# Attention pairs in hardware loops on five engines, in place of straight code

## The reference

```
for i in range(3):
    h  = (x @ W[i]).reshape(n, 4, 32)
    es, ed = einsum(h, att_src[i]), einsum(h, att_dst[i])
    e  = leaky_relu(es[src] + ed[dst], 0.2)
    p  = exp(e - segment_max(e, dst)[dst])
    alpha = p / segment_sum(p, dst)[dst]
    x  = elu(segment_sum(alpha[:, :, None] * h[src], dst) + bias[i])
```

## Time and profile before

| what | value |
|---|---|
| median of 3 runs | 9245.97 us (9245.64 to 9248.44) |
| profiled execution | 9241.63 us |
| its span, first to last instruction | 9239.8 us |
| first attention layer's gathers | 2079 to 4298 us |
| second's | 4450 to 6670 us |
| third's | 6856 to 9025 us |
| instructions executed | 129442 |

### The profile page before, as it was taken

One profiled execution on the slowest core, in us unless ns is written; L12 is line 12 of the kernel. 1 busy time (PEld: TensorE's weight loads), 2 busy tenths in 40 slices (PEclk: granted clock), 3 DMA queues, 4 the chain that ended last, 5 costly groups with the idle time before them and its releaser, 6 DMA issues.

```text
span 9239.8 us, 129442 instructions
## 1 busy us (share of the span) xinstructions
PE 5626.5 (61%) x34288; PEld 4513.0 (49%) x34288; DVE 5638.8 (61%) x13019; ACT 3271.8 (35%) x7522; POOL 5375.1 (58%) x5192
## 2 busy tenths in 40 slices
PE   4999879964555555555455555555534545445456
PEld 3777646653544445444444444454434444444444
DVE  6888721135666666666466666666645555555555
ACT  3555400023333333333343333333323333333334
POOL 2000100047777777775677777777657777777770
PEclk9999989965555555555555555555555555555558
DMA  3333335404444444443344444444423333233321
GB/s 101 136 139 139 125 140 192 175 16 120 119 119 116 122 113 124 114 116 82 96 113 118 119 116 121 113 123 113 104 65 80 85 80 85 79 85 80 85 79 32
DMA packets 601474, 989.07 MB, mean 107 GB/s; under 512 B 331107, under 2 KB 455044, under 8 KB 561524
## 3 DMA queue, kind: packets, MB, share of 16 engines
q0 software_dynamic: 163760, 357.05, 17.1%
q1 hardware_dynamic: 217540, 544.34, 16.8%
q10 hardware_dynamic: 219648, 81.82, 3.4%
HBM read 758.42 MB, written 224.34 MB: 106 GB/s over the span
## 4 chain that ended last, share of the span: by engine, by line
PE 27%; DVE 22%; DVEq 18%; POOL 14%; issue 13%; DMA 5%; ACT 1%; POOLq 0%; SPq 0%; ACTq 0%
DVEq L1264 15%; PE bank L959 13%; POOL arena L649 13%; DVE acc L1866 10%; DMA arena<-row_table,staged_idx 4%; PE bank L1182 3%; PE bank L984 3%; DVE arena L1853 2%; DVE arena L1822 2%; PE bank L1122 2%; DVEq L1866 2%; DVE x_mem L1535 1%; DVE arena L1815 1%; DVEq L1858 1%; PE bank L1247 1%
## 5 line engine op out<-in xcount | busy, mean ns | idle before, releaser
L649 POOL DMA_INDIRECT arena<-row_table,staged_idx x4992 | 5087.9, 1019 | 1626.1 <-issue 1467.3
L1182 PE MATMUL bank<-arena 128*128 128x136 f32 x9984 | 2487.9, 429 | 1207.5 <-DVE acc L1866 1045.8
L1182 PEld LDWEIGHTS bank<-arena 128*128 128x128 f32 x9984 | 2195.9, 316 | 1372.1 <-issue 1231.0
L1866 DVE TENSOR_TENSOR acc<-acc,bank 128x136 f32 x4992 | 1476.7, 296 | 1020.7 <-issue 798.1
L804 ACT ACTIVATE pick_dist<-col,dst_local 128x128 bf16<-128x128 f32 x4992 | 1523.3, 388 | 1092.0 <-PE bank L1182 1091.3
L959 PE MATMUL bank<-arena 128*128 128x385 bf16 (+1 forms) x7546 | 1342.6, 327 | 49.5 <-DVE arena L1639 33.0
L597 POOL TENSOR_TENSOR arena<-acc,node_stat 128x896 f32 x14 | 24.5, 1748 | 1721.8 <-POOLq L609 956.3
L959 PEld LDWEIGHTS bank<-arena 128*128 128x128 bf16 x7546 | 711.2, 98 | 476.5 <-DVE arena L1639 33.2
L1138 PE MATMUL bank<-ident,arena 128*32 128x128 f32 x624 | 161.5, 414 | 1206.8 <-DVE arena L1785 1206.8
L1853 DVE TENSOR_TENSOR arena<-arena,prob 128x528 f32<-128x528 f32 x1248 | 841.6, 695 | 0.2
L1782 DVE TENSOR_TENSOR arena<-arena 128x128 f32<-128x128 f32 x156 | 60.8, 390 | 1229.2 <-DMA arena<-row_table,staged_idx 1229.2
(11 more groups left out here) (354 smaller groups left out, 5383.0 us busy)
## 6 DMA issues: line engine op xcount, KB each, us to landing
arena<-dst_rows SPq DMA_DIRECT2D x156, 1024.0 KB
cell_rows<-arena SPq DMA_DIRECT2D x76, 1568.0 KB, 5.2
arena<-cell_rows SPq DMA_DIRECT2D x76, 1568.0 KB, 6.5
arena<-row_table,staged_idx POOLq DMA_INDIRECT x4992
edge_stats<-x_mem ACTq DMA_DIRECT2D x416, 192.0 KB, 3.5
x_mem<-in_edge_attr SPq DMA_DIRECT2D x208, 192.0 KB
x_mem<-segment_flags SPq DMA_DIRECT2D x416, 96.0 KB
arena<-change_rows SPq DMA_DIRECT2D x312, 64.0 KB
```

The costliest lines, as they stand in the source:

```text
L649: pool.indirect_dma_start(gathered[:, at, :], None, table, bass.IndirectOffsetOnAxis(staged_idx[:, at:at + 1], 0)).then_inc(att_gathered[n ...
L1182: mm = pe.matmul(region(k)[:, 0:ROW], pick[:, k, :], gathered[:, b * GROUP + k, :], start=True, stop=True)
L1866: done = dve.tensor_tensor(row, row, region(m * BATCH + k), ALU.add)
```

## The change

The loop over pairs becomes a hardware loop on each of the five engines. `it` is then a register, so each semaphore count and each slot number that depends on it is computed by register instructions inside the body. The last pair stays outside on all engines but POOL, whose loop holds all 26.

```diff
 # SP
-                for it in range(PAIRS - 1):
+                with sp.Fori(0, PAIRS - 1) as it:
 # GpSimd
-                for it in range(PAIRS):
+                with pool.Fori(0, PAIRS) as it:
 # ScalarE
-                for it in range(PAIRS - 1):
+                with act.Fori(0, PAIRS - 1) as it:
 # TensorE
-                for it in range(PAIRS - 1):
+                with pe.Fori(0, PAIRS - 1) as it:
 # VectorE
-                for it in range(PAIRS - 1):
+                with dve.Fori(0, PAIRS - 1) as it:
```

## The result

The changed kernel takes 9287.9 us (9281.7 to 9299.4, median of 4 runs), the kernel before in the same rounds 9245.8 (9244.5 to 9248.4). The ratio is 1.0046, 95% interval 1.0034 to 1.0058: 42 us slower. I had forecast 9238 and a range up to 9285. The profiled execution has a span of 9286.0 us, 46.2 more than before.

What follows compares the result with a forecast made beforehand. POOL's gathers, some held by VectorE's operations, bound the kernel. Looped groups of 42.6 us against 42.68 gave -8 us, the third layer 0: 9241.63 less 8 is 9234, plus 4.3 for the runs' median, forecast 9238, range 9135 to 9285.

Steps and rivals of the forecast that it cites:

- POOL is the bound, and all goes through the length of its gathers.: POOL paces the attention; a gather takes 0.944 us plus a 0.305 us gap, longer when VectorE's operations hold it.
- whoever comes second is blocked: On the ports that VectorE and POOL share under an exclusive lock, the later one is fully blocked; a gather took 1.47 us.
- In a loop each pair should be like the next. The even group is the one I take for it.: Looped groups would all resemble the 42.34 us one, plus 0.25: 42.6 against a mean of 42.68, -8 us over 100 groups.
- 43.96 us group of the earlier trace: Attention group ahead of the 42.34 us one, with the same instructions; taken as a sign that straight code's groups are uneven.
- VectorE's register instructions, 0.25 us per group.: Uncovered register instructions ahead of L1792, L1535, L1834 and the rescaling: 0.25 us per group, 0.2 to 0.9; third layer 0.15.
- a worse meeting: Slower rival: a later VectorE at L1769 holds gathers longer; +195 us if every group, 9290 if one in four; chance 0.18.
- POOL runs dry at the branch: Slower rival: VectorE's jump back stops its sequencer ahead of the rescaling, starving POOL; 9320 at a 7.4 us stop; chance 0.05.
- the condition in the prediction: A stop at VectorE's branch stays hidden up to 6.4 us per pair; each us above costs 75 us.
- 6.4 us of cover: POOL's sequencer wait ended at 3394.7 and opened the gather at 3401.1, 6.4 us later; a VectorE stop up to that stays hidden.
- TensorE, "Nothing": Branch 0.215 us per pair; the chain reopening POOL's rounds grows some 0.3 us, against 3.6 and 6.4 us: no cost.
- The scan escaped: Faster rival: L1535 starts behind its gather and holds it no more; group 41.6 us, -90 to -110 us, 9150; chance 0.30.
- the 0.23 that it needed: Delay of L1535 at 3428.35, in us, above which the gather comes first; 0.15 to 0.32 was expected.

Runs made afterwards that it cites:

- crossing_l1: The changed kernel with 0, 70 and 58 semaphore increments that nobody waits for ahead of VectorE's three layers: 9313.1 us, ratio 1.0067 to the kernel before.
- crossing_moved: The changed kernel with 58, 70 and 47 semaphore increments that nobody waits for ahead of VectorE's three layers: 9231.5 us, ratio 0.9982 to the kernel before.
- aligned_body: The changed kernel with 75, 70 and 47 semaphore increments ahead of VectorE's layers, so its loop body lies in three blocks: 9292.7 us, ratio 1.0054.
- straight_clear: The kernel before, with VectorE increments making each pair three blocks long, and 73, 7 and 95 ahead of the layers: 9236.4 us, ratio 0.9981.
- longer_stop_3: crossing_moved with 64 more increments at the top of VectorE's loop body, and 122, 6 and 111 ahead of the layers: 9572.2 us, ratio 1.0353.

## Why the prediction was wrong, by its steps

- **POOL is the bound, and all goes through the length of its gathers.** Right. Idle time per gather is unchanged (inside the layers only two gaps are longer than usual, 0.39 and 0.40 us), and 48.1 us of busy time stand for 46.2 of span. In these traces the lock works one way only, though: the prediction has it that whoever comes second is blocked, but VectorE's L1535 takes 1.28 us whether a gather is running when it begins (176 of 208 cases before) or not.
- **"In a loop each pair should be like the next. The even group is the one I take for it."** This is the step that failed. Pairs are alike, but the pauses between blocks are not smoothed away: they are nailed to three instructions. I had seen the 43.96 us group of the earlier trace rows, put it down to the uneven blocks, and then took it for something that a loop removes. The trace of before showed the cause already: L1799 was 0.36 us later in that group than in the even one. In fact the loop chose for each layer whether the long group occurs (almost) never or in every pair. It fell once in three loops on the good side (second layer, -12 us) and twice on the bad one (+28, +33).
- **VectorE's register instructions, 0.25 us per group.** Too much, and not what counted. Where no pause lies in between, L1792 to L1822 start 0.00 to 0.02 us later than before, and the first L1535 0.09 to 0.12 later (18.69 to 18.72 us after L1782, against 18.60 in the groups of before without a pause). The drains hide most of them. The 2.1 us per group by which L1782 waits less come from the stop behind the branch.
- **The rival "a worse meeting".** Right in kind, mechanism and nearly in size: I priced one group in four at 9290, and it was one in three, partly paid back by the good layer, at 9288; that the two times agree is luck. Its place was right (L1769), its cause not: not the register instructions ahead of L1792. At 0.18 it had too little.
- **The rival "POOL runs dry at the branch".** The stop that I gave 0.05 exists, 3.4 to 6.0 us, and stayed hidden as the condition in the prediction said. My 6.4 us of cover was too large: 5.1 us was the shortest lead of the round behind the branch in the kernel before, and the floor of 0.8 us goes off it.
- **TensorE, "Nothing".** Mis-sized. Against POOL's reopening nothing, but the scale goes by TensorE to VectorE's rescaling, and 0.10 us there cost 13 us by the same lock. The chain that I checked was the wrong one of two.
- **The scan escaped.** Right in mechanism and price, rare in the changed kernel. The delay of 0.09 to 0.12 us was under the 0.23 that it needed as a rule. The second L1535 let its gather go in 2 groups of the first layer and 6 of the second; seven of them took 41.5 to 41.7 us, as priced. In crossing_l1 it happened in 25 groups of the second layer.

The sum in retrospect: moving the pauses gave back 56 us (the changed kernel less crossing_moved); TensorE's loop costs 13 beside a straight VectorE. With both put right, the kernel with the loops of the other four is 27 us faster than straight code. Part of that is that the long groups of the straight code are gone too: over 43.5 us it had 5, 5 and none inside the three layers, this kernel none.

The Trainium skill (Runtime: NRT & Kernel Launch, Instruction fetch mechanics) says that engines but TensorE hold two blocks of 256 instructions, 512 in all, and that a branch out of them waits for a fetch. The trace agrees with the wait (3.4 us) and not with the size of a block, which is 128 instructions here (401 packets for 3.28 MB): a body of 375 instructions over four blocks is fetched anew, one over three is kept. The room for four blocks of 128 that theory H2 supposes would be the same 512 in all; no run shows it directly.

## What to carry to other kernels

Where an engine that shares a lock with the bound engine pauses every so many instructions, a loop fixes the pauses in place: look up where they fall, and shift the body by a few idle instructions before you judge the loop. (Fitting the body into fewer blocks took away the stop, but not the loss: that was aligned_body.) In straight code with a pass of whole blocks the same can be done, at about the same gain (straight_clear, 16 us less than before). And when a chain is called hidden, check each place where it touches the engine that holds the lock, not only the one where it reopens the bound.

## What the runs showed of the hardware

- VectorE's code comes in blocks of 128 instructions. A crossing costs some 0.35 us of sequencer time when the next block has just been fetched, 0.11 us when it has been there for whole iterations, and about 1.1 us at the first one behind the changed kernel's branch (second layer, body instruction 13).
- VectorE's body over four blocks is fetched anew in each iteration (five fetches per pair: 124 in 25 pairs) and stops 3.4 us behind its branch, 6.0 in the third layer, for which I have no reason; over three blocks it stays and costs 0.23 us.
- A gather that begins inside L1769 0.22 us ahead of its end gets in ahead of the next operation; 0.37 us ahead it is held through both. Around this point L1799 being 0.13 us late moved a group by 1.2 us (aligned_body, 43.95 against 42.80), while L1769 being 0.05 us late in its third layer left the gather's excess at 0.11 us.
- VectorE is not held by a gather that began before it: L1535 takes 1.28 us at the median with a gather running and without, at most 1.35.
- A semaphore increment that nobody waits for, shown as 21 ns, takes 93 ns of VectorE's sequencer when many stand in a row (longer_stop_3).
